# Transposes, Abs and Sign two steps at a time in a ternary quantisation pipeline

## The reference, cut to what matters

```python
def ternary_quant(w_fp32, g=64):
    w = w_fp32.astype(jnp.bfloat16)
    w_g = w.reshape(-1, g)
    scale = jnp.clip(jnp.mean(jnp.abs(w_g), axis=-1, keepdims=True), 1e-08, None)
    q = jnp.clip(jnp.round(w_g / scale), -1, 1)
    w_hat = (q * scale).reshape(w.shape)
    return w + jax.lax.stop_gradient(w_hat - w)

def ffn(x, w_gate_up, w_proj):           # w_gate_up 16384 x 2048, w_proj 2048 x 8192
    gate, up = jnp.split(x @ ternary_quant(w_gate_up).T, 2, axis=-1)
    return rms_norm(silu(gate) * up) @ ternary_quant(w_proj).T

x = x + 0.5 * ffn(layernorm(x), w_gate_up, w_proj)
x = x + windowed_attention(layernorm(x), wq, wk, wv, wo)
x = x + 0.5 * ffn(layernorm(x), w_gate_up, w_proj)
```

## Time and profile before

| | us |
|---|---|
| median of 3 runs | 7513.6 |
| the three runs | 7511.6, 7513.6, 7811.9 |
| profiled execution | 7529.7 |
| its span (first to last instruction, slowest core) | 7528.2 |
| spans of the eight cores | 7479.5 to 7528.2 |

### The profile page before, as it was taken

The page is one execution under the profiler, slowest core; times in us unless marked ns, Lnnn a source line. Parts: engine busy times, 40 slices in busy tenths (PEclk is TensorE's granted clock), DMA queues, the critical chain, the costliest instruction groups (busy, mean ns, idle before and its releaser), DMA issues.

```text
span 7528.2 us, 72875 instructions; the slowest of 8 cores (7479.5 to 7528.2 us)
## 1 busy us (share of the span) xinstructions
PE 5936.9 (79%) x24410; PEld 2329.1 (31%) x24410; DVE 2550.5 (34%) x4134; ACT 1592.8 (21%) x2589; POOL 883.5 (12%) x772
## 2 busy tenths in 40 slices
PE   5777777777765999999999992554666779999999
PEld 1122222212212443444444341232111334444434
DVE  3555555555553112211311204335444221131121
ACT  4444444444430000000000000001664000000000
POOL 2333343333440000000000000000000000000000
PEclk6555555555557999999999995787777889999999
DMA  4334434433323444444534342242001533354435
GB/s 136 134 135 140 141 137 141 143 139 135 134 90 119 150 161 165 155 147 149 183 149 157 136 170 92 76 134 56 0 0 30 172 120 149 139 186 145 146 141 161
DMA packets 270681, 976.85 MB, mean 130 GB/s; under 512 B 111473, under 2 KB 119794, under 8 KB 170994
## 3 DMA queue, kind: packets, MB, share of 16 engines
q1 hardware_dynamic: 253330, 882.01, 33.5%
q10 hardware_dynamic: 16992, 90.19, 3.5%
HBM read 835.81 MB, written 136.31 MB: 129 GB/s over the span
## 4 chain that ended last, share of the span: by engine, by line
PE 64%; DVE 16%; issue 9%; DMA 8%; ACT 2%; POOL 1%; SPq 0%; DVEq 0%; POOLq 0%; ACTq 0%
PE f_pg L718 15%; PE f_pu L718 15%; PE f_py L922 14%; DVE q_whb L478 6%; PE q_psS L379 5%; PE q_psTH L381 4%; PE a_py L1629 2%; DVE a_dsm L1541 1%; DMA cache_wp<-q_whb 1%; DMA q_nat<-wgu 1%; PE a_pq L1356 1%; DMA cache_gu<-q_whb 1%; PE a_pkv L1181 1%; DVE q_mm L465 1%; PE a_psd L1497 1%
## 5 line engine op out<-in xcount | busy, mean ns | idle before, releaser
L718 PE MATMUL f_pg<-f_xn,f_wgu 128*128 128x512 bf16 x5120 | 1147.2, 383 | 83.6 <-DVE f_xn L190 51.3
L922 PE MATMUL f_py<-f_h,f_wp 128*128 128x512 bf16 x5120 | 1130.0, 384 | 33.1 <-DVE f_h L736 13.9
L718 PE MATMUL f_pu<-f_xn,f_wgu 128*128 128x512 bf16 x5120 | 1146.3, 383 | 0.0
L503 POOL TENSOR_TENSOR q_tau<-q_mm,q_sig 128x512 bf16<-128x512 bf16 x768 | 883.3, 1150 | 1391.9 <-DVE q_mm L465 1309.8
L465 DVE TENSOR_TENSOR q_mm<-q_aT,q_psTH 128x512 bf16<-128x512 bf16 x768 | 528.8, 689 | 964.6 <-PE q_psTH L381 964.6
L733 DVE CAST f_u<-f_pu 128x512 bf16<-128x512 f32 x320 | 220.1, 688 | 1875.5 <-PE f_pu L718 1875.5
L379 PE MATMUL q_psS<-q_sg,sb_bsel 32*128 32x512 bf16 x768 | 446.0, 581 | 445.2 <-DVE q_whb L478 411.5
L718 PEld LDWEIGHTS f_pg<-f_xn,f_wgu 128*128 128x128 bf16 x5120 | 504.1, 99 | 702.6 <-issue 114.0
L922 PEld LDWEIGHTS f_py<-f_h,f_wp 128*128 128x128 bf16 x5120 | 503.5, 99 | 664.1 <-issue 91.7
L718 PEld LDWEIGHTS f_pu<-f_xn,f_wgu 128*128 128x128 bf16 x5120 | 504.7, 99 | 616.3 <-issue 51.2
L349 PE MATMUL q_psT<-sb_idn,q_natb 128*128 128x128 bf16 x3072 | 445.2, 306 | 249.2 <-DVE q_natb L287 196.1
(11 more groups left out here) (149 smaller groups left out, 3475.3 us busy)
## 6 DMA issues: line engine op xcount, KB each, us to landing
f_wgu<-cache_gu SPq DMA_DIRECT2D x320, 1024.0 KB, 6.9
q_nat<-wgu SPq DMA_DIRECT2D x32, 4096.0 KB, 18.2
f_wp<-cache_wp SPq DMA_DIRECT2D x90, 1024.0 KB, 8.2
f_wp<-cache_wp ACTq DMA_DIRECT2D x70, 1024.0 KB, 8.3
cache_gu<-q_whb SPq DMA_DIRECT2D x64, 1024.0 KB, 6.6
q_nat<-wp SPq DMA_DIRECT2D x16, 4096.0 KB, 16.1
cache_wp<-q_whb SPq DMA_DIRECT2D x64, 512.0 KB, 4.9
a_xnsb<-xn SPq DMA_DIRECT2D x44, 512.0 KB, 4.5
```

The costliest lines, as they stand in the source:

```text
L503: g.tensor_mul(tauv[:, pp, :], mmv[:, pp, :], sigv[:, i, :]).then_inc(b.gE.h, 1)
L718: _li = t.matmul(ps[:, :], wguv[:, sl, gu, i, hs * 128:(hs + 1) * 128], xnv[:, i, :], start=(i == 0), stop=(i == NDC - 1))
L922: _li = t.matmul(ps_y[par][:, 0:TT], wpv[:, sl, j, :], hv[:, j, :], start=(j == 0), stop=(j == 63))
```

## The change

Transposes, Abs and Sign work on packs of two steps. A pack pk stands for steps 2pk and 2pk+1.

- PE writes eight transposes into one `q_psT` buffer, all 1024 columns of it. The three buffers take turns by pack, and a pack waits for the Sign of three packs earlier.
- ACT runs one Abs and one Sign of 1024 columns for a pack: 16 instructions a set instead of 32. The two casts for the next set stand behind pack 3, so after step 7 as before.
- PE's order becomes: pack pk, bc(2pk-2), bc(2pk-1), gsum(2pk-4), gsum(2pk-3). At the end of a set stand bc(14), bc(15) and gsum(12) to gsum(15).
- gsum(i) waits for the Abs of pack i//2, the last for the last Sign. q_tau(i) waits for the Sign of pack i//2.

bc, gsum, q_mm, q_tau, q_whb, the casts and all DMAs keep their sizes and counts. The diff, with the order for the first set and the unchanged casts cut:

```diff
--- before.py
+++ after.py
@@ -314,11 +314,11 @@
 
                 emb_k = (cur is not None) and (k + 1 < nsets)
 
-                def s_abs(S0_, i, emb):
-                    return S0_ + 2 * i + 1 + (2 if (emb and i >= 8) else 0)
-
-                def s_sign(S0_, i, emb):
-                    return s_abs(S0_, i, emb) + 1
+                def s_abs(S0_, pk, emb):
+                    return S0_ + 2 * pk + 1 + (2 if (emb and pk >= 4) else 0)
+
+                def s_sign(S0_, pk, emb):
+                    return s_abs(S0_, pk, emb) + 1
 
                 v_base = V0 + (4 if prv is not None else 0)
 
@@ -333,31 +333,34 @@
                 gs_rec = {}
                 sl = k % 2
 
-                def emit_tr(i):
+                def emit_tr(pk):
                     @blk.tensor
-                    def _(t, i=i, sl=sl, vck=cast_vc[k], sck=cast_sc[k],
+                    def _(t, pk=pk, sl=sl, vck=cast_vc[k], sck=cast_sc[k],
                           pS0=prevS0, S0=S0, emb=emb_k, pemb=prev_emb):
-                        if i == 0:
+                        if pk == 0:
                             t.wait_ge(b.vE.h, vck)
                             t.wait_ge(b.sE.h, sck)
-                        if i >= 3:
-                            t.wait_ge(b.sE.h, s_sign(S0, i - 3, emb))
+                        if pk >= 3:
+                            t.wait_ge(b.sE.h, s_sign(S0, pk - 3, emb))
                         elif pS0 > 0:
                             t.wait_ge(b.sE.h,
-                                      s_sign(pS0, 13 + (i + 2) % 3, pemb))
-                        for r in range(4):
-                            _li = t.transpose(ps_T[i % 3][:, r * 128:(r + 1) * 128],
-                                              natbv[:, sl, r, i * 128:(i + 1) * 128],
-                                              C["idn"][:, :])
+                                      s_sign(pS0, {0: 6, 1: 7, 2: 5}[pk], pemb))
+                        for ii in (2 * pk, 2 * pk + 1):
+                            for r in range(4):
+                                _li = t.transpose(
+                                    ps_T[pk % 3][:, (ii % 2) * 512 + r * 128:
+                                                 (ii % 2) * 512 + (r + 1) * 128],
+                                    natbv[:, sl, r, ii * 128:(ii + 1) * 128],
+                                    C["idn"][:, :])
                         _li.then_inc(b.tE.h, 1)
-                    tr_rec[i] = b.tE.inc()
+                    tr_rec[pk] = b.tE.inc()
 
                 def emit_gsum(i):
                     @blk.tensor
                     def _(t, i=i, sp=sp, sgr=sg_read, S0=S0, emb=emb_k,
                           aTv=aTv_[:, sp]):
-                        t.wait_ge(b.sE.h, s_sign(S0, 15, emb) if i == 15
-                                  else s_abs(S0, i, emb))
+                        t.wait_ge(b.sE.h, s_sign(S0, 7, emb) if i == 15
+                                  else s_abs(S0, i // 2, emb))
                         if i == 0:
                             if sgr > 0:
                                 t.wait_ge(b.vE.h, sgr)
@@ -383,48 +386,54 @@
                     bc_rec[i] = b.tE.inc()
 
                 if cur is not None and prv is not None:
-                    for i in range(16):
-                        emit_tr(i)
-                        if i >= 2:
-                            emit_bc(i - 2)
-                        if i >= 3:
-                            emit_gsum(i - 3)
+                    for pk in range(8):
+                        emit_tr(pk)
+                        for j in (2 * pk - 2, 2 * pk - 1):
+                            if 0 <= j < 16:
+                                emit_bc(j)
+                        for j in (2 * pk - 4, 2 * pk - 3):
+                            if 0 <= j < 16:
+                                emit_gsum(j)
                     emit_bc(14)
                     emit_bc(15)
-                    for i in (13, 14, 15):
+                    for i in (12, 13, 14, 15):
                         emit_gsum(i)
...
                 if cur is not None:
                     gsum_last = gs_rec[15]
-                    slot_free[sl] = tr_rec[15]
+                    slot_free[sl] = tr_rec[7]
 
                 if cur is not None:
                     @blk.scalar
                     def _(s, S0=S0, sp=sp, kk=k, atV=aT_freeV[sp], emb=emb_k,
-                          trp=[tr_rec[i] for i in range(16)],
+                          trp=[tr_rec[pk] for pk in range(8)],
                           sgf=list(sig_freeG[sp]), sigv=sigv_[:, sp],
                           aTv=aTv_[:, sp]):
-                        for i in range(16):
-                            s.wait_ge(b.tE.h, trp[i])
-                            if i == 0 and atV > 0:
+                        for pk in range(8):
+                            s.wait_ge(b.tE.h, trp[pk])
+                            if pk == 0 and atV > 0:
                                 s.wait_ge(b.vE.h, atV)
-                            li = s.activation(aTv[:, i, :], ps_T[i % 3][:, 0:512],
-                                              AF.Abs)
+                            li = s.activation(aTv[:, 2 * pk:2 * pk + 2, :],
+                                              ps_T[pk % 3][:, :].rearrange(
+                                                  "p (a f) -> p a f", a=2), AF.Abs)
                             li.then_inc(b.sE.h, 1)
-                            if sgf[i] > 0:
-                                s.wait_ge(b.gE.h, sgf[i])
-                            s.activation(sigv[:, i, :], ps_T[i % 3][:, 0:512],
+                            if sgf[2 * pk + 1] > 0:
+                                s.wait_ge(b.gE.h, sgf[2 * pk + 1])
+                            s.activation(sigv[:, 2 * pk:2 * pk + 2, :],
+                                         ps_T[pk % 3][:, :].rearrange(
+                                             "p (a f) -> p a f", a=2),
                                          AF.Sign).then_inc(b.sE.h, 1)
-                            if i == 7 and emb:
+                            if pk == 3 and emb:
...
-                    b.sE.inc(32 + (2 if emb_k else 0))
+                    b.sE.inc(16 + (2 if emb_k else 0))
                     if emb_k:
-                        cast_sc[k + 1] = S0 + 18
-                    assert b.sE.n == s_sign(S0, 15, emb_k)
+                        cast_sc[k + 1] = S0 + 10
+                    assert b.sE.n == s_sign(S0, 7, emb_k)
 
                 if prv is not None:
                     @blk.vector
@@ -497,7 +506,7 @@
                         def _(g, i=i, pp=i % 2, pv=pv, pS0=prevS0,
                               pemb=prev_emb, sigv=sigv_[:, pv]):
                             g.wait_ge(b.vE.h, v_m(i))
-                            g.wait_ge(b.sE.h, s_sign(pS0, i, pemb))
+                            g.wait_ge(b.sE.h, s_sign(pS0, i // 2, pemb))
                             if i >= 2:
                                 g.wait_ge(b.vE.h, v_wh(i - 2))
                             g.tensor_mul(tauv[:, pp, :], mmv[:, pp, :],
```

## The result

The changed kernel takes 1.0113 times as long as the kernel before, 95% interval 1.0093 to 1.0132, which is 70 to 99 us more; the forecast was 63 more, just under that interval, and "within 2%" was given 0.92. The others took 7581.8 to 7622.3 us, with a median of 7588.9, where 7577 was forecast for it; those of the kernel before took 7509.4 to 7529.7. The profiled execution took 7581.8 us, its span is 7580.2.

A forecast was written before the change was run, and what follows sets the result against it. The prediction took the 2.55 us circle q_psS, q_psTH, q_mm, q_whb on PE and DVE as the bound. 5 x 0.31 - 0.20 = 1.35 us a set over 47 sets added 63 us to the 7513.6 median: 7577 us, range 7500 to 7630.

The forecast's parts named there:

- The stage and the bound: Whole program: only the quantisation stage's 48 sets can move, paced by a PE and DVE circle, granted clock staying 0.50.
- the circle: PE and DVE, each step: q_psS, q_psTH, q_mm, q_whb, next q_psS; 2.55 us, leaving PE 2.17 us from q_psTH.
- ACT at zero: ACT's Abs and Sign: halving the instructions saves only idle time, 0 us; without idle time at most 9.7 us a set.
- The upper bound: ACT, one 1024-column instruction: at most two of today's 512-column ones, 1.21 us, against 1.04 by the slope.
- the lower one: ACT, one 1024-column instruction: at least the 0.61 us of a 512-column one.
- The price of a place: PE between bc(odd) and bc(even): two gsums and eight transposes take 2.47 us against 2.17, costing 0.31 each.
- Five places: PE after bc(3), (5), (7), (9) and (11), where two gsums and a pack follow: 1.55 us a set.
- The start of a set: PE's bc(0) and bc(1) follow each other, so q_whb(0) waits only for q_tau(0): gain taken as 0.20 us.
- The sum: Quantisation stage: 5 x 0.31 - 0.20 = 1.35 us a set, times 47 overlapping sets, 63 us more.
- A: Rival, PE: the excess vanishes and only the start's gain is left, -9 us, 7504 us; chance 0.10.
- C: Rival, ACT: back too late from its casts, so gsum(8) and pack 7 wait; 7670 us at 10 us; chance 0.03.
- B: Rival, PE: longer runs raise the clock; single rises 7500 us, chance 0.06; throughout 7248 us, chance 0.04.

The follow-up runs named there:

- e2_wide_act_fine: Against the kernel before: ACT's wide instructions of 1024 columns, PE's old order of four transposes, gsums one step later; a set of 45.95 us.
- e3_gsum_moved: Changed kernel with one gsum of each pair moved between bc(even) and bc(odd), packs of eight transposes kept; a set of 45.95 us.
- e4_extra_tight: Changed kernel with four extra transposes five times a set, right behind bc(odd) and before the gsums; a set of 50.4 us, 7726 us in all.
- e1_narrow_act_packed: Changed kernel's PE order, with ACT's old 32 instructions of 512 columns a set; a set of 47.69 us.
- e7_thfirst_fine: e2_wide_act_fine with q_psTH issued before q_psS, each with its own wait; ratio 0.9425 to the kernel before, a set of 37.0 to 37.4 us.

## Why the prediction was right

**The stage and the bound.** Right. Only the quantisation stage moved, at the same granted clock, and the circle that was read from the earlier trace rows is what a step waits for: PE's work behind q_psTH cost nothing at 1.62 and 2.06 us, under the 2.17 that the circle leaves (`e2_wide_act_fine`, `e3_gsum_moved`), and above it every further us cost its full length (`e4_extra_tight`); and when the circle was cut the step fell from 2.55 to PE's own 2.04.

**ACT at zero.** Right, and shown: with the order undone the wide instructions left the set at 45.95 us. The duration by the slope, 1.04, was measured at 1.02 to 1.03. The upper bound, two narrow instructions, changed nothing (`e1_narrow_act_packed`, 47.69); the lower one wasn't tried. What the prediction adds for a kernel whose ACT has no idle time, up to 9.7 us a set, is far too much, as two stretches without idle time show, before and then after:

```profile
1031.43 0.60 ACT L420 ACTIVATE q_aT<-q_psT 128x512 bf16<-128x512 bf16 x1
1031.92 0.59 ACT L425 ACTIVATE q_sig<-q_psT 128x512 bf16<-128x512 bf16 x1
```

```profile
1016.67 1.02 ACT L426 ACTIVATE q_aT<-q_psT 128x1024 bf16<-128x1024 bf16 x1
1017.59 1.02 ACT L432 ACTIVATE q_sig<-q_psT 128x1024 bf16<-128x1024 bf16 x1
```

Neighbours overlap: narrow ones start 0.48 to 0.49 us apart, wide ones 0.90 to 0.92. By the starts, two wide ones in place of four save about 0.1 us a pack, so an estimate from these rows is 0.8 us a set, were ACT the limit.

**The price of a place.** Right in kind, 0.31 for 0.34. The gap is 2.49, not 2.47, because the eight transposes take 0.96 to the next q_psS and not 0.94; and where q_psS follows PE's own work without a wait, q_psTH starts 0.40 behind it and not 0.38 (1025.85 to 1026.25, against 1022.99 to 1023.36). This second term was missing in the sum, though the q_psS at 1033.18 of before was one of that sort; its q_psTH follows 0.40 behind. Five places: 1.7 instead of 1.55.

```profile
1033.58 0.63 PE L381 MATMUL q_psTH<-q_thb,sb_bsel 32*128 32x512 bf16 x1
```

**The start of a set.** Right in kind, 0.12 for 0.20. q_whb(0) did move up to where q_tau(0) leaves it, but it started 0.18 after q_tau's end (1018.28 + 1.15 to 1019.61) and not 0.1.

**The sum.** 1.6 us a set instead of 1.35, 47 x 1.6 = 75 instead of 63, and the stage measured 76 in the mean of the cores. The rest of the sum, casts, gsums at the end, first and last set at zero, holds in these profiles. So the mechanism was right, and both of its terms erred the same way, toward too small a loss.

**The rivals.** A, no excess: fell. C, gsum waiting for ACT: fell; the casts end 22 us into the set as before. B, the clock: fell, and further than I had reason to say. I had argued from runs of 3.9 us. In `e7_thfirst_fine` PE was busy 24.7 of 25.1 us without a wait over 0.3, and the granted clock stayed at 0.50. Those with 32 rows were 25 of its 88 matmuls and filled 0.96 of the 2.04 us of a step:

```profile
1006.10:1031.20 25.10, 24.68 (x88) 7.55 (x87) 16.02 (x25) 16.41 (x16) 14.18 (x13) 0.50 0.53 176
```

By the rule of the Trainium skill (TensorE: Matmul & The Clock Gate, "Part 1: The HAM clock gate"), that sustained activity releases the throttle, this stretch should have run at the upper level; the trace disagrees. In every kernel profiled here, on every core, the granted clock reads 0.50 from 63 us on to the end of the stage. Whether it is the rows in use that matter was not tried by itself, and the cause stays open.

## What to carry to other kernels

Before work is grouped on an engine, measure the gap that each group will stand in: from the release of the engine to the point at which the critical circle next needs it. Busy share over a stage doesn't answer that, since PE had 28% of it idle and the change still cost time; the same four transposes were free in one gap and paid in full in the next. And where two instructions of one engine feed a circle, issue first the one whose result starts the circle's next link, with its own wait: that reordering was worth 3.8% alone and 5.7% together with the wide Abs and Sign, where halving an idle engine's instructions without it was worth nothing. When such an order is priced, the start and the end of a set have to be priced too: that was left out in three expectations here, and their sets were 2 to 4 us too long.

## What the runs showed of the hardware

- TensorE stayed at the lower clock level (granted clock 0.50) through 25.1 us with no pause over 0.3 us (`e7_thfirst_fine`), in a mix of matmuls with 128 and with 32 rows; in the first set of the kernel before, stretches of 128-row matmuls alone were followed by the upper level, in which four transposes took 0.40 us and not 0.61.
- An Abs or Sign of 128x1024 bf16 from PSUM takes 1.03 us and one of 128x512 takes 0.61, but without idle time between them they start 0.91 and 0.48 us apart.
- A q_psTH whose q_psS didn't have to wait starts 0.40 us behind it, otherwise 0.37 to 0.38.
